# Stores behind the last load, TensorE's branch behind the stores, and another order in the tail of a masked-attention kernel

## The reference, cut to what matters

```python
h = jnp.maximum(_layernorm(x), 0.0)          # x: 4096 x 128 fp32
H = h @ W_fc + b_fc                          # 4096 x 128
s_src, s_dst = H @ w_att[:128], H @ w_att[128:]
scores = s_src[:, None] + s_dst[None, :] + b_att
scores = jnp.where(adj > 0, scores, -1e9)    # adj: 4096 x 4096 int32
out = x + softmax(scores, axis=1) @ H
```

## Time and profile before

| | |
|---|---|
| median of 3 runs | 180.94 us (180.92 to 181.69) |
| the profiled execution's own time | 181.24 us |
| its span, first to last instruction | 179.5 us |
| TensorE (PE) busy | 153.8 us, 86% |
| VectorE (DVE), ScalarE (ACT) busy | 121.2 us, 83.9 us |
| moved over DMA | 71.65 MB, mean 399 GB/s |
| mean granted TensorE clock | 0.976 |

### The profile page before, as it was taken

One profiled execution on the slowest core, in us unless ns is written; L12 is line 12 of the kernel. 1 busy time (PEld: TensorE's weight loads), 2 busy tenths in 40 slices (PEclk: granted clock), 3 DMA queues, 4 the chain that ended last, 5 costly groups with the idle time before them and its releaser, 6 DMA issues.

```text
span 179.5 us, 2952 instructions
## 1 busy us (share of the span) xinstructions
PE 153.8 (86%) x992; PEld 127.8 (71%) x992; DVE 121.2 (68%) x348; ACT 83.9 (47%) x249; POOL 10.0 (6%) x32
## 2 busy tenths in 40 slices
PE   0629947998769999999989999995999999799980
PEld 0327625666357777666667999995999999799960
DVE  0995695937999854988878656754576493755740
ACT  2568894999477143222226224435025444144140
POOL 2104301000050020000000000000000000000000
PEclk9999999999978999999999999999699999999998
DMA  6999999999999999999999999999999999999932
GB/s 137 404 442 433 409 436 438 416 427 435 420 431 435 418 420 436 424 427 435 415 425 425 427 420 422 430 425 422 419 433 427 410 419 424 418 420 399 387 116 66
DMA packets 8947, 71.65 MB, mean 399 GB/s; under 512 B 993, under 2 KB 1762, under 8 KB 3810
## 3 DMA queue, kind: packets, MB, share of 16 engines
q1 hardware_dynamic: 8352, 71.18, 95.1%
q10 hardware_dynamic: 578, 0.26, 0.6%
HBM read 69.34 MB, written 2.10 MB: 398 GB/s over the span
## 4 chain that ended last, share of the span: by engine, by line
DMA 68%; DVE 13%; PE 8%; issue 4%; ACT 2%; SPq 2%; DVEq 0%; ACTq 0%
DMA ring<-adj 68%; DVE mask L608 7%; PE bank L996 7%; DVE features L630 1%; DVE weighted L841 1%; ACT mask L518 1%; PE bank L1126 1%; DVE mask L616 1%; PE bank L1073 1%; ACT weighted L432 1%; SPq L331 1%; DVE high_bits L709 1%; DVE sums_T L735 1%; SPq L337 0%; DVE x_sb L830 0%
## 5 line engine op out<-in xcount | busy, mean ns | idle before, releaser
L608 DVE TENSOR_SCALAR mask<-ring 128x1536 fp32r<-128x1536 int32 (+2 forms) x69 | 63.9, 942 | 39.4 <-DMA ring<-adj 36.5
L996 PE MATMUL bank<-features,mask 128*128 128x258 f32 x512 | 67.2, 290 | 3.0 <-DVE mask L608 2.8
L996 PEld LDWEIGHTS bank<-features,mask 128*128 128x128 f32 x512 | 64.2, 194 | 4.6 <-DVE mask L608 4.0
L518 ACT ACTIVATE mask<-ring,half_steep 128x512 fp32r<-128x512 int32 x41 | 27.8, 718 | 58.2 <-DMA ring<-adj 58.2
L969 PE MATMUL bank<-mask,features 128*128 128x512 f32 x128 | 39.0, 429 | 10.3 <-DVE mask L608 5.5
L969 PEld LDWEIGHTS bank<-mask,features 128*128 128x128 f32 x128 | 24.3, 201 | 22.7 <-DVE mask L608 10.2
L974 PE MATMUL bank<-mask,features 128*128 128x512 f32 x128 | 36.6, 409 | 0.0
L974 PEld LDWEIGHTS bank<-mask,features 128*128 128x128 f32 x128 | 25.3, 198 | 6.1
L432 ACT ACTIVATE weighted<-relu,w_over_std 128x128 f32<-128x128 f32 x32 | 10.1, 390 | 4.4 <-DVE w_over_std L701 4.3
L443 ACT ACTIVATE relu<-x_sb,neg_mean 128x128 f32<-128x128 f32 x32 | 9.8, 388 | 3.1 <-DVE neg_mean L639 3.1
L742 DVE SCALAR_TENSOR_TENSOR x_sb<-bank,inv_den,x_sb 128x128 f32<-128x128 f32 x28 | 8.0, 343 | 4.4 <-PE bank L1049 4.4
(11 more groups left out here) (99 smaller groups left out, 94.7 us busy)
## 6 DMA issues: line engine op xcount, KB each, us to landing
ring<-adj SPq DMA_DIRECT2D x15, 2048.0 KB, 17.4
ring<-adj SPq DMA_DIRECT2D x15, 1536.0 KB, 13.3
ring<-adj SPq DMA_DIRECT2D x9, 1024.0 KB, 14.3
out<-x_sb SPq DMA_DIRECT2D x7, 256.0 KB, 10.2
ring<-adj SPq DMA_DIRECT2D x2, 768.0 KB, 11.8
x_sb<-x SPq DMA_DIRECT2D x1, 1024.0 KB, 20.4
ring<-adj SPq DMA_DIRECT2D x4, 256.0 KB, 17.1
x_sb<-x SPq DMA_DIRECT2D x2, 256.0 KB, 3.7
```

Of the source, the lines that this page charges most:

```text
L518: nc.scalar.activation(mask[:, n % MASKS, cols - part:cols], ring[:, n // 2 % RING, begin + cols - part:begin + cols], ACT.Sigmoid, bias=h ...
L608: nc.vector.tensor_scalar(mask[:, n % MASKS, 0:cols], ring[:, n // 2 % RING, begin:begin + cols], 0.0, None, ALU.is_gt).then_inc(masks_rea ...
L996: last = nc.tensor.matmul(bank[:, BANKS[g][b], 0:WIDE], mask[:, n % MASKS, at:at + P], features[:, t, :, :].rearrange("p h d -> p (h d)"), ...
```

## The change

Three edits. SyncE waits for the last load (`last_landed[3]`) before its first store. TensorE waits for all 11 stores between the load of its flag and its branch. And in the tail the four transposes come first, then the four products: T0 T1 T2 T3 P0 P1 P2 P3.

```diff
                 sp.dma_start(ring[:, LAST_PAIR % RING, cols], last_pair[:, cols]).then_inc(last_landed[i], 16)
+
+            sp.wait_ge(last_landed[PARTS - 1], 16)
             for k in range(BLOCKS):
                 sp.wait_ge(results_ready, k + 1)
...
             for m in range(LAST_TILES):
                 pe.wait_ge(last_parts_added, m + 1)
                 nc.tensor.transpose(bank[:, BANKS[LAST_GROUP][m], 0:P], sums[:, m, 0:D], ident[:]).then_inc(turned, 1)
-                if m >= 2:
-                    last_product(m - 2)
-            for m in range(LAST_TILES - 2, LAST_TILES):
+            for m in range(LAST_TILES):
                 last_product(m)
 
             pe.wait_ge(path_chosen, 1)
             general = pe.value_load(flag[0:1, 0:1], min_val=0, max_val=1)
+
+            pe.wait_ge(out_stored, 16 * STORES)
             with pe.If(general != 0):
```

## The result

The changed kernel took 179.64 us, median of 5 runs (179.5 to 180.14), against 180.94 us (180.8 to 181.69, also 5 runs): a ratio of 0.9922, interval 0.9897 to 0.9947, that is 0.8% faster. The forecast was 179.1. The span of the profiled execution went from 179.5 to 177.6 us; the sum had given 177.57.

The account below looks back on a forecast made before the run. TensorE was the bound until its last matmuls, with 4.15 us after the last arithmetic; the terms took the span from 179.45 to 177.57, -1.9 us, so 180.94 became 179.04, stated as 179.1, range 178.7 to 181.3.

Parts of the forecast that it names:

- The hold: End of block: TensorE's branch packet delays the final store; waiting for all stores gives back 2.1 us.
- the branch's cost: After the final store's landing: TensorE's branch and DRAIN are no longer hidden, so the new wait costs 0.34 us.
- Moved stores: SyncE's stores behind the last load: no load delayed, no gain from earlier loads, 0.05 us charged.
- the drain: Transfer of the seven large stores: 1.84 MB at 404 GB/s take 4.55 us, from 170.45 to 175.0.
- the slack of 0.5 us: Before the small stores: SyncE's first one moves no packets before 175.48, while the large stores drain at 175.0.
- the slack of 1.0 us: Before the final store: its packets are due at 176.0; each us of lateness beyond 1.0 costs a us.
- Order in the tail: Tail: T3 runs in TensorE's idle time ahead of P0; gain 0.17 us, limited by VectorE.
- B: Rival, chance 0.17: TensorE or what follows the program needs the fetched instructions, so the fetch moves to the end; 181.3 us.
- C: Rival, chance 0.12: another fetch, a q14 packet of VectorE or ScalarE, holds the final store; 180.3 us.
- D: Rival, chance 0.08: stores too late through slow issues, 191 us; mild form, transfer at 300 GB/s, 179.7 us.
- A: The forecast itself, chance 0.55: 178.7 to 179.6 us.
- E: Rival, chance 0.08: the branch change does nothing, q8 isn't what held the nine packets; 181.1 us.

Follow-up runs that it names:

- flag after results: Kernel before with the new tail order, and TensorE waiting for VectorE's last result before loading its flag, no store wait: 178.94 us, ratio 0.9899.
- stores only: Kernel before with only SyncE's stores moved behind the last load: 179.50 us, ratio 0.9914.
- stores and order: Changed kernel without TensorE's wait for all stores: 179.49 us, ratio 0.9915.
- later stores: Changed kernel with SyncE's wait put on the last result of the third group in place of the last load: 180.90 us, ratio 1.0002.

## Why the prediction was right, point by point, and where it was not

**The hold.** Right, and the main term. Of the 4.15 us between the last arithmetic and the end, 2.1 were nine packets of the final store behind an instruction packet of TensorE (no branch, no q8 packet, no hold). Of the two sides of TensorE's wait, the final store went from 3.7 to 1.6 us when the wait came alone, and the branch's cost came out as priced: 0.7 us from the landing (174.94 + 2.0 = 176.9) to the end (177.6), against 0.77.

**Which edit brings it.** The text put the whole gain on TensorE's wait and gave the moved stores nothing. The wait is enough; but the moved stores are enough too, by a way that I had not seen: with them the load of the flag takes 0.87 to 0.94 us in place of 0.49, and the branch falls behind the final store's issue. The prediction said of that load only that it "stands before the wait and stays hidden"; it did not ask what the moved stores do to its length, and that length decides which comes first, the branch or the issue. It also named no rival by which the moved stores bring the gain. The two edits don't add up, as each removes the same hold: 0.7% and 0.9% alone, 0.8% together.

**Moved stores.** Mechanism right, size wrong. I charged 0.05 us, and 0.3 to 0.4 are measured (small stores at 1.9 to 2.0 us for 1.6; 179.64 against 179.33 us with the stores left early). The term at fault is the drain. The packets of the seven stores ran from 170.18 to 175.7, where I had 170.45 to 175.0; 1.84 MB in 5.5 us are about 330 GB/s (my estimate), for the assumed 404. Each issue took 0.34 to 0.73 us and not 0.33; whether the issues or the transfer set that pace is not shown. So the slack of 0.5 us was gone, and the slack of 1.0 us that I gave the final store was none either: its packets shared full engines with those of the three other small stores, and its last packet moved at 176.55. That loads would not pay was right: the last mask starts 1.54 us after TensorE's last block of matmuls began at 167.80, as before (169.56 - 168.01 = 1.55).

**Order in the tail.** Right: from first addition to last result 0.19 us less, 0.17 forecast. Alone it brings nothing, since the hold goes by the branch.

**The number.** On the profiled executions 181.24 became 179.50, 1.74 less, for 1.9 forecast; the misses nearly cancel (stores +0.3; tail begun 0.2 sooner by chance; branch and end 0.1 less). That the span of 177.6 us hit the forecast of 177.57 so closely is partly luck. The medians moved by 1.3 us. I had taken the whole 1.9 off the median. But the profiled execution of before lay 0.30 above its median and that of after 0.14 below, which are 0.44 of the 0.6 that are missing.

**The rivals.** B: nothing waited for the packet at the end. The DRAIN followed the end of the branch by 0.05 to 0.07 us in all thirteen traces that have the branch, and in the changed kernel the program was over before the packet was recorded, so nobody needed it. C: in the changed kernel both q14 packets came at 177 us or later, after the last packet of a store; whose they are, no run shows, only that they are there without TensorE's branch. D in its mild form happened beside A: about 330 GB/s where it had 300 and A 404. The 179.64 us lie just above A's own range, 178.7 to 179.6, and next to mild D's 179.7. E is excluded by the kernel with the wait only and the one without the branch, both with the final store at 1.6 us.

## What to carry to other kernels

When the last arithmetic ends well before the span, count the packets of the final store by window: nine that come apart from 135 point to one DMA engine that did something else. If that is the instruction packet of an engine's last branch, put the branch well behind the issue of the last store: 1.0 us was free, while 0.3 us, seen only with the stores late, had one run of ten at the old time. A wait for the last result ahead of the load of the flag does it for nothing (178.94 us); a wait for the landing of all stores costs the branch itself, 0.3 to 0.4 us (179.33 us). And an edit can work by shifting something that it doesn't name, so undo it in company as well as try it alone.

## What the runs showed of the hardware

- A branch of TensorE at the time of a store's issue, 0.0 us apart, let that store's packets on one DMA engine come late (3.3 us from issue to landing for 1.6); 0.3 us behind it (late stores) or 1.0 us behind it (early stores) it did not. In the kernel before, the other engines had moved their packets of the final store by 176.5, the q8 packet was recorded only from 177.03 on, and its engine moved none of its nine until 178.03. The 0.99 us of the q8 packet itself don't explain the time before 177.03. What the engine does between the request and the packet is not visible in the traces.
- TensorE's load of one flag into a register took 0.48 to 0.49 us in the kernels with early stores, whether the DMA engines were idle (before) or busy for 0.91 of the time (flag after results). It took 0.87 to 1.08 us at the same place in those with moved stores (changed, stores only, stores and order, later stores), and 0.73 us with late stores and the flag loaded early.
- In the changed kernel the DMA engines were busy for only 0.21 and 0.14 of the time at 167 to 169 us (80 and 37 GB/s), and the last mask still waited for its load until 169.34. So the last share of the loads came late and slowly; 0.21 and 0.14 of 16 engines are 3.4 and 2.2 at a time on average.
- The kernel before itself was at 179.11 us in one of 29 runs of one session, and at 179.10 us in one of 23 of another. That would fit runs in which the branch fell behind the issue; no trace of them was taken.
